# A tuned transformer layer on one core: VectorE forms the sum U4 ahead of the low part of the last group's probabilities

## The reference, cut to what matters

```python
q, k, v = proj(Q, Wq, bq), proj(K, Wk, bk), proj(V, Wv, bv)      # K = V = the context, 25088 x 512
scores = jnp.einsum('bhqd,bhkd->bhqk', q, k) / jnp.sqrt(jnp.float32(DK))
attn = jax.nn.softmax(scores, axis=-1)
out = jnp.einsum('bhqk,bhkd->bhqd', attn, v)
```

## Time and profile before

| | |
|---|---|
| time, median of 3 runs | 1660.45 us (1659.76 to 1660.83) |
| the profiled execution | 1662.99 us, span 1661.3 us |
| PE busy | 1566.8 us, 94% of the span |
| DVE busy | 1323.7 us, 80% |
| ACT busy | 1268.4 us, 76% |
| POOL busy | 822.6 us, 50% |

### The profile page before, as it was taken

How to read it: one execution, slowest core, us unless ns; L and a number is a source line. 1 busy time by engine, 2 the same in 40 slices (tenths; PEclk the granted TensorE clock), 3 DMA queues, 4 the chain that set the end, 5 groups by cost and what they waited for, 6 DMA issues and landing times.

```text
span 1661.3 us, 47795 instructions
## 1 busy us (share of the span) xinstructions
PE 1566.8 (94%) x17748; PEld 1276.5 (77%) x17748; DVE 1323.7 (80%) x1764; ACT 1268.4 (76%) x3074; POOL 822.6 (50%) x938
## 2 busy tenths in 40 slices
PE   7899999999999999999999999999998687999998
PEld 5788888888888888888888888888876455777776
DVE  7788888888888888888888888888887466766765
ACT  4888888888888888888888888888886254655554
POOL 5667657666676576666765766667653000000000
PEclk9999999999999999999999999999999765999999
DMA  4365454454544544545445445454456630555551
GB/s 171 80 136 129 107 139 112 122 133 108 137 126 107 139 110 123 134 111 134 126 107 139 111 123 133 108 137 126 109 106 157 167 151 1 191 204 210 192 198 43
DMA packets 442690, 216.03 MB, mean 130 GB/s; under 512 B 416768, under 2 KB 422912, under 8 KB 436112
## 3 DMA queue, kind: packets, MB, share of 16 engines
q1 hardware_dynamic: 442352, 215.07, 48.1%
q10 hardware_dynamic: 288, 0.27, 0.1%
HBM read 111.96 MB, written 0.56 MB: 68 GB/s over the span
## 4 chain that ended last, share of the span: by engine, by line
DVE 33%; PE 25%; ACT 20%; issue 18%; DMA 1%; SPq 1%; DVEq 1%; ACTq 0%; POOL 0%; POOLq 0%
ACT prob L573 14%; DVE cmax L839 12%; PE ps_proj L1316 9%; DVE p_s L852 6%; DVE nmax L846 5%; PE ps_o L1339 5%; PE ps_proj L1147 4%; ACT p_s L584 3%; DVE k_s L864 2%; DVE ps_proj L877 2%; DVE v_s L861 2%; PE ps_s L1193 2%; ACT v_s L549 1%; PE ps_proj L1176 1%; PE ps_s L1272 1%
## 5 line engine op out<-in xcount | busy, mean ns | idle before, releaser
L1147 PE MATMUL ps_proj<-ctx_s,wk_s 128*128 128x256 f16 x4032 | 487.9, 273 | 30.5 <-DVE ps_proj L877 27.6
L1147 PE MATMUL ps_proj<-wv_s,ctx_s 128*128 128x256 f16 x4032 | 483.5, 274 | 1.2 <-ACT ps_proj L529 1.2
L1147 PEld LDWEIGHTS ps_proj<-ctx_s,wk_s 128*128 128x128 f16 x4032 | 376.5, 98 | 103.7 <-issue 63.1
L1147 PEld LDWEIGHTS ps_proj<-wv_s,ctx_s 128*128 128x128 f16 x4032 | 381.3, 98 | 64.6 <-issue 20.0
L573 ACT ACTIVATE prob<-ps_s,nmax 128x256 f32<-128x256 f32 x784 | 360.4, 473 | 77.0 <-DVE nmax L846 72.5
L380 POOL TENSOR_TENSOR ctx_s<-t_f,ctx_s 128x512 f16<-128x512 f32 x192 | 220.0, 1157 | 358.9 <-ACT ctx_s L475 358.9
L852 DVE SCALAR_TENSOR_TENSOR p_s<-prob,p_s 128x1024 f16<-128x1024 f32 x196 | 291.1, 1485 | 57.6 <-ACT p_s L584 57.6
L839 DVE TENSOR_REDUCE cmax<-ps_s 128x4 f32<-128x1024 f32 x196 | 238.1, 1215 | 3.8 <-PE ps_s L1193 3.8
L584 ACT ACTIVATE p_s<-prob 128x1024 f16<-128x1024 f32 x196 | 209.1, 1067 | 6.7
L380 POOL TENSOR_TENSOR ctx_s<-ctx_f,ctx_s 128x512 f16<-128x512 f32 x144 | 167.1, 1160 | 69.2 <-ACT ctx_s L470 69.2
L1316 PE MATMUL ps_proj<-x_s,wsp 128*128 128x256 f16 x1536 | 180.5, 275 | 4.2 <-issue 3.2
(11 more groups left out here) (163 smaller groups left out, 1875.5 us busy)
## 6 DMA issues: line engine op xcount, KB each, us to landing
ctx_f<-ctxt_dram SPq DMA_DIRECT2D x48, 1024.0 KB, 5.1
wst<-w_dram SPq DMA_DIRECT2D x96, 512.0 KB, 4.7
pt_s<-p_s SPq DMA_TRANSPOSE x392, 2.7
w_in_sb<-w_in_dram SPq DMA_DIRECT2D x1, 3072.0 KB, 11.1
tisa<-tisa_scores SPq DMA_DIRECT2D x3, 1024.0 KB, 12.0
w_f<-wk_dram SPq DMA_DIRECT2D x2, 512.0 KB, 5.7
ctx_f<-ctxt_dram SPq DMA_DIRECT2D x2, 512.0 KB, 7.0
w_f<-wv_dram SPq DMA_DIRECT2D x1, 1024.0 KB, 9.9
```

Of the source, the lines that this page charges most:

```text
L1147: ins = pe.matmul(ps_proj[:, bank(h, role), sub * QUARTER:(sub + 1) * QUARTER], lhsT, rhs, start=(fresh and sub == 0 and t == 0 and i == 0 ...
```

## The change

In VectorE's step, `add_u4` is called ahead of `p_lows` of the group before, and no longer behind it. No instruction is added or removed, and the other engines' programs are the same.

```diff
                     if exists(c, 0):
                         maxima(c, 2 * h, odd)
+                    if strassen:
+                        add_u4(c + 1, h)
                     pc, pg = back(c, 2 * h, 1)
                     if exists(pc, 0):
                         p_lows(pc, pg)
-                    if strassen:
-                        add_u4(c + 1, h)
                     if exists(c, -1):
                         add_o(c - 1, h)
```

## The result

| | before | after |
|---|---|---|
| time, median of 6 runs each | 1660.64 us | 1678.67 us |
| ratio | | 1.0107, 95% interval 1.0093 to 1.0121 |
| span of the profiled execution | 1661.3 us | 1677.8 us |
| period of a chunk, over 32 and 31 chunks | 25.56 us | 25.90 us |

The period is taken from the starts of GpSimd's L363, which runs once a chunk: after the change (1110.32 - 307.43) / 31 = 25.90 us, before it (1122.61 - 304.75) / 32 = 25.56 us.

A forecast was written before the change was run, and what follows sets the result against it. Bound: the chain of exponentials, TensorE's scores and M5, high parts, GpSimd's L380 and nmax, not M7's wait for U4. 45 x 0.33 = 14.9 us on 1660.45 gave 1675.3 us; range 1657 to 1687.

The forecast's parts named there:

- The wait removed is not on the chain: TensorE's M7 waits for U4 in h = 0, 0.60 us a chunk; claimed not to set the period.
- U4 waits for M6 for 0.78 us: VectorE, h = 0: U4 now needs only M6, and VectorE idles 0.78 us ahead of it.
- L368 goes first and the low part is held: h = 0: GpSimd's L368 goes ahead of group 3's low part on VectorE, leaving VectorE 0.565 us later.
- The first L380 is held, 1.49 us: GpSimd, h = 0: group 0's low part holds the first L380, about 1.5 us instead of 1.16.
- the handover with overlap: L380 held in h = 0, ending 0.155 us sooner than whole durations in turn: 0.33 us a chunk.
- the whole 0.48 us: L380 held in h = 0 for whole instructions without overlap: 0.48 us a chunk, 21.6 us in all.
- The last wait hides the rest: h = 0: nmax of group 1 still ends with GpSimd's pair, so 0.33 of VectorE's 0.565 us arrive.
- The transpose would be late and hidden: h = 0: group 3's low-part transpose lands at 748.2, `weigh` waits for it, at no cost.
- h = 1 costs nothing: h = 1: VectorE is 0.15 us late, but nmax of group 3 ends as before with L380; no cost.
- The sum: Whole kernel: 45 chunks x 0.33 us = 14.9 us added.
- The faster rival: h = 0: low part goes ahead of L368, nmax may slip in, TensorE becomes the bound: 1628 us, 14%.

The follow-up runs named there:

- the run with `add_o` behind: Kernel after the change, with the low part of group 0 moved ahead of `add_o` in h = 0: 1665.29 us, ratio 1.0018.
- moving nmax alone: Kernel before the change, with the maxima of group 1 moved ahead of the first low block in h = 0: 1652.99 us, ratio 0.9945.
- the kernel with the late sum: Kernel after the change, with GpSimd's fourth context sum (L368) moved behind the half's first three low parts: 1625.55 us, ratio 0.9782.
- its own run: Kernel before the change, with U4 put ahead of the low part in h = 1 (values) only: 1661.11 us, ratio 0.9992.
- the move of GpSimd's sum: Kernel before the change, with only GpSimd's fourth context sum moved behind the first three low parts: 1661.68 us, ratio 1.0001.

## Why the prediction was right, step by step

- **The wait removed is not on the chain.** Right: in the run with `add_o` behind the wait is gone and the period is the old one. But it was next in line: moving nmax alone gives 0.18 us a chunk until M7's wait sets the period. That is about all that TensorE waited for the exponentials in the kernel before: a gap of 0.10 us ahead of the scores of group 2, where in the kernel with the late sum the two rows overlap by 0.07 us, 0.17 us in all.
- **U4 waits for M6 for 0.78 us.** Measured 0.75 us; U4 starts 751.00, 0.15 us after M6's end at 748.06 + 2.79 = 750.85.
- **L368 goes first and the low part is held.** Forecast: low part about 2.1 us, L368 1.28 us. Measured 2.11 and 1.27 us. Their issues are 0.25 us apart, forecast 0.29. The reading behind it, "the one that was issued first goes first", was a little too sharp: in the earlier trace rows the low part's row begins at 741.69 and L366's at 741.70, and L366 went first. VectorE's row begins 0.08 us before the instruction ahead of it ends (741.77), so the starts of rows settle the order only to about 0.1 us. The margin here was larger than that, but not by much.
- **The first L380 is held, 1.49 us.** Measured 1.51 us. Of the two readings the handover with overlap (0.33 us) was right, and the whole 0.48 us was not: the period rose by 0.34 us. The Trainium skill (SBUF — State Buffer, Who interferes with whom) says that where the two engines contend, the one that issues first blocks the other for the whole instruction. The trace agrees on who holds whom, but the row of the instruction that waits ends some 0.15 us sooner than whole durations one after the other would have it (L380 at 756.64, and not at 755.62 + 1.16 = 756.78). The Trainium skill says in the same section that a VectorE instruction with at most one SBUF input does not contend with GpSimd, outside the two-port modes. The trace agrees: `add_u4`, with one input in PSUM, took 0.88 us for its two instructions here, with L368 issued in the midst of them and done in its usual 1.27 us, and 0.87 us before.
- **The last wait hides the rest.** Right, and tested: with L380 free, nmax of group 1 takes 0.37 us in place of 0.90, still ends with the pair, and the period is back.
- **The transpose would be late and hidden.** Right: 0.41 us of wait, and free in the run with `add_o` behind. It costs about 0.40 us a chunk once the exponentials come sooner.
- **h = 1 costs nothing.** Right, by its own run.
- **The sum.** 45 x 0.342 = 15.4 us, forecast 14.9. The span rose by 16.5 us: 15.0 us up to the last L368 (1231.4 to 1246.4 us), and 1.5 us behind it, where the forecast had put nothing. The medians differ by 18.0 us, with an interval of 15.4 to 20.1 us by the ratio, so the forecast of 14.9 us is a little low: besides the end, the profiled execution lay 2.4 us above the median before and only 0.9 us after.
- **The faster rival** was mis-sized: TensorE's slack, taken as 25.57 - 24.86 = 0.71 us from the busy time, came out as 0.85 to 0.89 us (25.56 less the periods of 24.71 to 24.67 us). Where TensorE does not wait, a matmul row overlaps the next by some 0.07 us, and where it waits that overlap is missing, so busy time counts more than the engine needs. Its condition, the low part ahead of L368, did not come true; its price was tried in the kernel with the late sum.

One sentence above needs its limit: that nmax waits for GpSimd and GpSimd for the low part is read from the order of issue and the durations in eleven kernels, and no run changed where the inputs lie.

## What to carry to other kernels

A wait of the busiest engine is worth its length only if nothing else ties the loop; look for the second place at which that engine would wait, and follow that chain round once before moving anything. Where VectorE and GpSimd take turns, a move of a few tenths of a microsecond decides who goes first, and the price can appear further on, on the other engine: L368 went first, and GpSimd's next instruction, L380, was held in turn. When a reordering loses, the same reordering with the neighbour moved out of its way may win: the exchange cost 1.1% by itself, the move of GpSimd's sum was worth nothing by itself, and together they gave 2.2%.

## What the runs showed of the hardware

These are the sizes in this kernel. A VectorE instruction of 1.21 us with both inputs in SBUF took 2.37 us behind one GpSimd sum and 2.11 us behind another, and one on four columns, 0.16 us at its shortest, took up to 0.95 us in this stretch. A GpSimd sum of 1.27 us held in its turn ended 1.12 us after the VectorE instruction, and one of 1.16 us ended 1.02 us after it.

Between two GpSimd instructions back to back the four-column instruction could get in: issued in the first it ended with the first, issued in the second it ended with the pair. Moving the maxima so that it got in was worth 25.90 - 25.19 = 0.71 us a chunk in the kernel after the change, and in the kernel before it only 0.18 us, since another wait of TensorE was next.
